# Fused decoder layer: GpSimd rounds and subtracts the pieces of the second expert matrix in visits 1 to 7

## What is computed

```
logits = einsum('bsh,eh->bse', x, Wg);  Sm = swapaxes(softmax(logits), 1, 2)
G, I = top_k(Sm, K)                      # K = 128 = all tokens of a sequence
h1  = gelu(einsum('bekh,ehf->bekf', ex, W1) + b1[None, :, None, :])
out = einsum('bekf,efh->bekh', h1, W2) + b2[None, :, None, :]
```

## Time and profile before

| | |
|---|---|
| time, median of 3 runs | 1049.42 us (1047.12 to 1050.45) |
| the profiled execution | 1047.37 us |
| its span in the trace | 1045.7 us |
| PE, PEld busy | 939.9 us (90%), 846.1 us (81%) |
| DVE, ACT busy | 645.8 us (62%), 608.4 us (58%) |
| POOL busy | 88.5 us (8%) |

### The profile page before, as it was taken

The page is one execution under the profiler, slowest core; times in us unless marked ns, Lnnn a source line. Parts: engine busy times, 40 slices in busy tenths (PEclk is TensorE's granted clock), DMA queues, the critical chain, the costliest instruction groups (busy, mean ns, idle before and its releaser), DMA issues.

```text
span 1045.7 us, 17612 instructions
## 1 busy us (share of the span) xinstructions
PE 939.9 (90%) x6480; PEld 846.1 (81%) x6480; DVE 645.8 (62%) x1334; ACT 608.4 (58%) x1039; POOL 88.5 (8%) x117
## 2 busy tenths in 40 slices
PE   5548786988799989999899989999899989999997
PEld 4447686877688888888798888988798888889997
DVE  6767767885567646675566636675556646343665
ACT  6347675665555555556565555556565565454675
POOL 2012001100120001100111001100011001000000
PEclk9569988999899999999999999999999999999999
DMA  6067879754644445445453445354444444565350
GB/s 203 11 211 250 269 265 295 251 181 153 201 141 143 140 151 163 146 136 157 140 178 121 150 157 161 123 166 133 149 149 154 143 142 146 178 197 159 113 178 11
DMA packets 143541, 170.32 MB, mean 163 GB/s; under 512 B 11080, under 2 KB 110688, under 8 KB 143456
## 3 DMA queue, kind: packets, MB, share of 16 engines
q1 hardware_dynamic: 143456, 169.19, 50.7%
HBM read 133.50 MB, written 35.65 MB: 162 GB/s over the span
## 4 chain that ended last, share of the span: by engine, by line
PE 70%; DVE 14%; ACT 11%; issue 3%; DMA 0%; POOL 0%; SPq 0%; POOLq 0%; ACTq 0%; DVEq 0%
PE up_ps L444 10%; PE up_ps L446 10%; PE up_ps L445 10%; PE down_ps L658 9%; PE down_ps L659 9%; PE down_ps L660 9%; PE bank L444 3%; PE bank L445 2%; PE bank L446 2%; DVE w_lo L835 2%; DVE h_lo L835 2%; ACT L717 2%; ACT probs L717 2%; DVE pt_lo L915 2%; DVE kd L865 2%
## 5 line engine op out<-in xcount | busy, mean ns | idle before, releaser
L771 ACT ACTIVATE h_all<-up_ps,b_all 128x512 f32<-128x512 f32 (+1 forms) x296 | 182.4, 630 | 358.2 <-PE up_ps L446 354.9
L658 PE MATMUL down_ps<-w_hi,h_hi 128*128 128x256 f32 x1024 | 297.9, 291 | 32.2 <-DVE h_lo L835 32.2
L659 PE MATMUL down_ps<-w_lo,h_hi 128*128 128x256 f32 x1024 | 292.2, 285 | 0.0
L660 PE MATMUL down_ps<-w_hi,h_lo 128*128 128x256 f32 x1024 | 292.0, 285 | 0.0
L835 DVE TENSOR_TENSOR h_lo<-h_all,h_hi 128x512 fp32r<-128x512 f32 x256 | 184.8, 723 | 172.3 <-ACT h_hi L762 171.8
L658 PEld LDWEIGHTS down_ps<-w_hi,h_hi 128*128 128x128 f32 x1024 | 197.7, 193 | 44.1 <-issue 32.1
L444 PE MATMUL up_ps<-x2t_hi,w_hi 128*128 128x512 f32 (+1 forms) x592 | 224.3, 379 | 0.0
L445 PE MATMUL up_ps<-x2t_lo,w_hi 128*128 128x512 f32 (+1 forms) x592 | 219.5, 371 | 0.0
L446 PE MATMUL up_ps<-x2t_hi,w_lo 128*128 128x512 f32 (+1 forms) x592 | 219.4, 371 | 0.0
L659 PEld LDWEIGHTS down_ps<-w_lo,h_hi 128*128 128x128 f32 x1024 | 198.4, 194 | 5.4
L660 PEld LDWEIGHTS down_ps<-w_hi,h_lo 128*128 128x128 f32 x1024 | 198.3, 194 | 0.0
(11 more groups left out here) (171 smaller groups left out, 1106.4 us busy)
## 6 DMA issues: line engine op xcount, KB each, us to landing
w_hi<-w_parts SPq DMA_DIRECT2D x192, 256.0 KB, 3.1
w_lo<-w_parts SPq DMA_DIRECT2D x192, 256.0 KB, 3.3
w_raw<-in_w_dram SPq DMA_DIRECT2D x104, 256.0 KB, 3.4
w_parts<-w_hi SPq DMA_DIRECT2D x64, 256.0 KB, 3.6
w_parts<-w_lo SPq DMA_DIRECT2D x64, 256.0 KB, 4.2
x_in<-in_x_dram SPq DMA_DIRECT2D x8, 256.0 KB, 4.4
ctx_sb<-in_ctx_dram SPq DMA_DIRECT2D x8, 256.0 KB, 4.5
out_dram<-acc SPq DMA_DIRECT2D x8, 256.0 KB, 2.6
```

The costliest lines, as they stand in the source:

```text
L658: nc.tensor.matmul(ps, hi, w2h[:, c, :], start=c == 0 and j == 0, stop=False, skip_group_check=True)
L659: nc.tensor.matmul(ps, hi, w2l[:, c, :], start=False, stop=False, skip_group_check=True)
L660: mm = nc.tensor.matmul(ps, lo, w2h[:, c, :], start=False, stop=c == FC - 1 and j == PAIR - 1, skip_group_check=True)
L771: a = nc.scalar.activation(h_all[:, unit % HALL, k * wide:(k + 1) * wide], up_ps[unit % 2][:, k * wide:(k + 1) * wide], ACT.Gelu_apprx_tan ...
```

## The change

For the pieces of W2 of visits 1 to 7 (28 pieces) the new function `split` on GpSimd does both the rounding and the subtraction; ScalarE and VectorE leave them out. The waits are those that ScalarE had, with one on GpSimd's own earlier subtraction (`w2_ready`), since both semaphores must rise in the order of the pieces. The split stands behind the other work of its item in GpSimd's order. The four pieces of visit 0 and the pieces of visits 32 to 36 stay where they were, and so do all pieces of W1.

```diff
+    def by_pool(n, i):
+        return i == 1 and 0 < n < E
...
                     for visit, i, q in splits(n, k):
-                        split_hi(visit, i, q)
+                        if not by_pool(visit, i):
+                            split_hi(visit, i, q)
...
                     for visit, i, q in splits(n, k):
-                        split_lo(visit, i, q)
+                        if not by_pool(visit, i):
+                            split_lo(visit, i, q)
...
+            def split(n, q):
+
+                m = sequence(n, 1, q)
+                pool.wait_ge(raw_loaded[m % RAW], 16 * (m // RAW + 1))
+                pool.wait_ge(down_done, last_reader(n - 1, q) + 1)
+                pool.wait_ge(kept[1][q], 16 * 2 * n)
+                pool.wait_ge(w2_ready, G * n + q)
+                nc.gpsimd.tensor_copy(piece(w2_hi, 1, q), raw(m, 1)).then_inc(w2_hi_ready, 1)
+                pool.wait_ge(w2_hi_ready, G * n + q + 1)
+                nc.gpsimd.tensor_tensor(piece(w2_lo, 1, q), raw(m, 1), piece(w2_hi, 1, q).bitcast(F32), ALU.subtract)\
+                    .then_inc(w2_ready, 1)
...
+                    for visit, i, q in splits(n, k):
+                        if by_pool(visit, i):
+                            split(visit, q)
```

## The result

The changed kernel takes 1056.65 us (median of 4 runs, 1055.81 to 1058.80) against 1049.68 us for the kernel before on the same chip: 1.0074 times, 95% interval 1.0051 to 1.0097. The forecast was 3.3 us faster.

A forecast was written before the change was run, and what follows sets the result against it. PE was taken to bound the kernel from 270 us on, with some 33 us of idle time before. Savings of 7.8 us less 4.5 us for GpSimd and DVE stopping each other gave 3.3 us: 1046.1 us, range 1041 to 1053.

The forecast's parts named there:

- the eight waits that the prediction priced one by one: PE's waits from 91.77 to 269.41 us with W2 pieces in their chain, each given a saving of 0.5 to 1.2 us.
- 160.65: PE's wait for `h_lo` at 160.65 us, behind a W2 piece's rounding and subtraction: 0.52 + 0.6 = 1.1 us saved.
- the sum: Savings in PE's waits between 70 and 270 us, six small ones included: 7.8 us gross; other waits given nothing.
- the last rival: All 7.8 us arrive and PE's clock holds in visits 0 to 4: -11 us, 1038 us; chance 0.08.
- ACT's share: Part of the 7.8 us path saving from ScalarE's 28 removed roundings: about 2.8 us.
- DVE's: Part of the path saving from VectorE's 28 removed subtractions: about 5 of 16.8 us.
- On the path it is weighed like the savings: ... 30%: Of the 15 us that GpSimd's pieces cost DVE, 30% was taken to reach PE's path: 4.5 us.
- the mechanism of the prediction: A DVE instruction with two SBUF operands and GpSimd exclude each other; one reading PSUM does not; a full hit costs 1.1 us.
- the prediction's own 15 us of stall: DVE time lost to GpSimd's 28 moved pieces: 28 x 0.55 = 15 us, nearly all of the 16.8 freed.
- The price of a piece: DVE time lost to each piece on GpSimd: 0.4 us for the subtraction and 0.15 us for the cast.
- the lock costs more than it frees: Rival, in DVE's unbroken rows: +1.5 to +6.5 us, about 1053, deciding from 0.93 us lost per piece; chance 0.20.
- Order on GpSimd and SP: `v_cat`, queued behind pieces, ends some 6 us later within 8.6 us of cover; SP's store and reload costed at nothing.

The follow-up runs named there:

- e1: The changed kernel, but GpSimd rounds and subtracts only 4 of each piece's 512 columns, same order and waits: 1038.29 us, -10.5 us against the kernel before.
- e4: The changed kernel, but ACT rounds the 28 pieces again and GpSimd only subtracts them: 1056.43 us, +7.7 us against the kernel before.
- e6: ACT rounds whole pieces as in the kernel before; GpSimd subtracts only 4 of 512 columns of the 28, the rest left out: 1040.89 us, -8.9 us.
- e7: The kernel before plus 56 GpSimd fills that read nothing, at the changed kernel's places and waits: 1054.68 us, +4.9 us.
- e2: The kernel before plus 28 casts and 28 subtractions on GpSimd scratch tiles, at the changed kernel's places and waits: 1070.54 us, +21.8 us.
- e5: DVE subtracts whole pieces as in the kernel before; GpSimd rounds only 4 of 512 columns of the 28, the rest left out: 1046.13 us, -3.7 us.

## Why the prediction was wrong

**What bounds, the relief.** The reading of PE's waits held, place by place. In e1, which has the relief without the stall, the eight waits that the prediction priced one by one shrink by 0.60, 0.45, 0.52, 0.67, 1.22, 0.37, 0.86 and 0.59 us: 5.3 of the 6.0 that were given for them, and 160.65, called the clearest, is the one most overrated (0.67 for 1.1).

All waits together shrink by 4.6, mainly since one that the sum left out grows: that for the second `exp_k`, 3.25 us at 280.10 before, is 4.87 at 269.42 in e1. So in PE's waits the relief was 4.6 us and not 7.8. The time fell by 10.5 all the same, because PE's granted clock rose with it (0.93 to 0.96, 6.5 us of busy time in the traces). The forecast had nothing for this; it stood in the last rival alone, which gave 1038 us and got 0.08. That 7.8 and 10.5 lie near each other is luck.

By the times, ACT's share was put at 2.8 and measured 3.7; DVE's was put at 5 and measured 8.9 (the two together are more than e1's 10.5; that both stand in some of the same waits would explain it, and was not tested). In the changed kernel itself the wait of 160.65 is 1.51 us (at 164.64), 2.4 less than before, but in e1 only 0.67 of this is relief; the rest I put down to the longer waits ahead of it, and no run tests that.

**The step that failed** is "On the path it is weighed like the savings: ... 30%". A stall is not spread over DVE's time as the removed pieces were. By the mechanism of the prediction it can only fall on DVE where DVE is working on SBUF, and that, as I read it, is mostly in the unbroken rows that PE waits for. Measured: 86% of the stall is in the time, in two pairs of kernels (17.5 of 20.3 us, 21.8 of 25.4), 75% for the subtractions alone (e4 against e6). PE's waits by themselves take 11.7 of the 20.3 us, 58%, and 15.5 of the 25.4, 61%; most of the rest goes with PE's lower clock (5.6 and 4.7 us of busy time). With 86% the prediction's own 15 us of stall would be 13, and 7.8 - 13 is a loss of 5: this one share turned the sign. The other way round, 30% of the measured 20.3 us are 6, less than the relief.

**The price of a piece** was put at 0.55 us (0.4 and 0.15) and measured 0.73. The full hits came about as often as forecast: 14 DVE instructions are 0.8 to 1.1 us longer beside a piece, one for every second piece, where 0.4 us a piece stood for ten. Two parts of the price were missed. `kd`, the norm's `y` and the small `att` were left out, because no row of the kernel before showed one of them beside GpSimd; `kd` alone went from 480 to 649 ns, its 32 from 13.4 to 19.0 us of busy time. And three pieces that become ready close together (116 to 122 us) hit the same row one after another. The rival that had the sign right, "the lock costs more than it frees", named the mechanism and the place, and put its deciding point at 0.93 us a piece on the same 30%; with the measured relief and share I estimate it at 10.5 / 0.86 / 28 = 0.44 us.

**The rule of the Trainium skill** ("Perfetto Trace Analysis", "Optimizing Scalar/DVE Operations") that moving work between these two engines might not help was given less weight than the trace's undisturbed cases. The result agrees with it: 28 pieces moved cost 7.0 us.

**Order on GpSimd and SP.** Right to cost nothing in the changed kernel. `v_cat` of pair 1 ends at 102.2 there (101.05 + 1.17), 8.3 us later and not some 6, and PE takes it at 104.60: the cover fell from 8.6 to 2.4 us and held. e1 excludes the order by itself as the cause, and e7 leaves at most 4.9 of e2's 21.8 us for order and length together.

**Open.** How much of the relief and of the 86% is PE's clock is known from one trace of each kernel only. The granted clock was higher where PE waited less (0.96, 0.93 and 0.91 in e1, the kernel before and e2), but not always: the changed kernel, with 7 us more waiting than the kernel before, has 0.94, and so has e5, with the same waiting as before.

## What to carry to other kernels

Before work goes from a busy engine to GpSimd, count what VectorE does at the moments when that work would run: here instructions that stay on SBUF were held up by as much as 1.1 us by a GpSimd subtraction of 1.27 us, and those that read PSUM were not. Weigh relief and stall apart: relief counts where the freed piece happens to stand in a chain, here a quarter to a half of it, while a stall can only fall on a working VectorE, and here three quarters or more of it arrived. Look at PE's busy time as well as at its waits: part of both came and went with its clock. If work must go there, hold it back with a semaphore until VectorE turns to PSUM; six pieces placed so won 2.7 us where twenty-eight unplaced ones lost 7.

## What the runs showed of the hardware

- A GpSimd fill, which reads nothing, holds up a one-input DVE instruction from SBUF to SBUF (`kd`, 480 to 678 ns on average) and not a two-input one (708 to 719 ns). GpSimd instructions that read hold up both (629 and 884 ns).
- A waiting GpSimd subtraction took its turn between two DVE instructions that were both ready, in 116 to 122 us twice in a row. The cast that waited 1.6 us for a gap, in the earlier trace rows, was not the rule: the 28 casts average 0.79 us in the changed kernel, 0.18 over the undisturbed 0.61.
- On GpSimd a cast of 128x512 to fp32r takes 0.61 us undisturbed and a subtraction of fp32r from float32 1.27 us, against 0.64 and 1.15 us for the rows that they were estimated from.
